# Up chunks 0 and 1 as a fourth seven-product pair in the last two token blocks, kept in DRAM in between

## The reference

```
xn = layernorm(x)
s  = silu(xn @ w_gate.T);  the k = 1376 smallest |s| of each token are set to 0
a  = (s * (xn @ w_up.T)) @ w_down.T
h  = relu(xn @ up_w) ** 2
r  = ((xn @ fc1_w) @ expert_w.T) * (sum of the 2 largest of xn @ gate_w)
y  = x + a + layernorm(h @ down_w + r @ fc2_w) * gamma + beta
```

## Time and profile before

| | us |
|---|---|
| median of 3 runs | 2335.4 |
| lowest, highest | 2333.67, 2336.62 |
| the profiled run, its own time | 2335.83 |
| its span in the trace | 2333.7 |
| TensorE busy | 2317.7 |
| VectorE busy | 1634.8 |
| ScalarE busy | 1086.9 |
| GpSimd busy | 829.3 |

### The profile page before, as it was taken

One profiled execution on the slowest core, in us unless ns is written; L12 is line 12 of the kernel. 1 busy time (PEld: TensorE's weight loads), 2 busy tenths in 40 slices (PEclk: granted clock), 3 DMA queues, 4 the chain that ended last, 5 costly groups with the idle time before them and its releaser, 6 DMA issues.

```text
span 2333.7 us, 27748 instructions
## 1 busy us (share of the span) xinstructions
PE 2317.7 (99%) x10504; PEld 1927.2 (83%) x10504; DVE 1634.8 (70%) x1810; ACT 1086.9 (47%) x1253; POOL 829.3 (36%) x682
## 2 busy tenths in 40 slices
PE   8999999999999999999999999999999999999999
PEld 6888888888877888888888888888888888888887
DVE  4349999976265989897334598898723568989850
ACT  3247776223233787722124387761213448785110
POOL 5467878796444021123024321304004413030500
PEclk9999999999999999999999999999999999999999
DMA  7798878878898666665778766665667865556555
GB/s 277 280 394 294 292 245 311 293 243 310 287 363 302 206 196 191 204 201 180 234 237 277 249 194 193 195 209 189 207 219 255 279 221 195 193 192 214 180 190 180
DMA packets 191047, 558.43 MB, mean 239 GB/s; under 512 B 20161, under 2 KB 29377, under 8 KB 190913
## 3 DMA queue, kind: packets, MB, share of 16 engines
q1 hardware_dynamic: 190912, 556.65, 71.0%
HBM read 429.62 MB, written 126.94 MB: 238 GB/s over the span
## 4 chain that ended last, share of the span: by engine, by line
PE 93%; DMA 3%; DVE 1%; SPq 1%; POOL 1%; ACT 0%; issue 0%; DVEq 0%; ACTq 0%
PE bank L945 30%; PE bank L947 30%; PE bank L946 30%; PE bank L965 2%; DMA mixed_w<-mixes 1%; DMA split_w<-w 1%; DMA w<-mixed_w 1%; PE bank L956 1%; POOL w L732 0%; SPq L565 0%; SPq L569 0%; PE bank L1038 0%; PE bank L1039 0%; DMA raw<-w_gate_dram 0%; POOL w L735 0%
## 5 line engine op out<-in xcount | busy, mean ns | idle before, releaser
L1292 DVE TENSOR_SCALAR_CACHE_REDUCE junk_v<-mag,cand 128x2816 bf16<-128x2816 f32 x248 | 780.3, 3146 | 8.8
L786 ACT ACTIVATE junk_s<-mag,cand 128x2816 uint8<-128x2816 f32 x248 | 655.4, 2643 | 222.2 <-DVE cand L1284 195.7
L945 PE MATMUL bank<-w,tok 128*128 128x512 f32 (+1 forms) x952 | 365.8, 384 | 1.8 <-DMA w<-split_w 1.7
L947 PE MATMUL bank<-w,tok 128*128 128x512 f32 (+1 forms) x952 | 364.3, 383 | 0.0
L946 PE MATMUL bank<-w,tok 128*128 128x512 f32 (+1 forms) x952 | 364.1, 382 | 0.0
L732 POOL TENSOR_TENSOR w<-raw,w 128x512 fp32r<-128x512 f32 (+1 forms) x196 | 268.1, 1372 | 77.5 <-ACT w L774 67.8
L945 PE MATMUL bank<-w,prod_t 128*128 128x512 f32 x672 | 269.4, 401 | 0.0
L947 PE MATMUL bank<-w,prod_t 128*128 128x512 f32 x672 | 262.8, 391 | 0.0
L946 PE MATMUL bank<-w,prod_t 128*128 128x512 f32 x672 | 261.9, 390 | 0.0
L945 PE MATMUL bank<-tok,w 128*128 128x512 f32 x640 | 249.0, 389 | 0.0
L946 PE MATMUL bank<-tok,w 128*128 128x512 f32 x640 | 249.0, 389 | 0.0
(11 more groups left out here) (149 smaller groups left out, 3728.3 us busy)
## 6 DMA issues: line engine op xcount, KB each, us to landing
w<-split_w SPq DMA_DIRECT2D x516, 512.0 KB, 3.5
split_w<-w SPq DMA_DIRECT2D x192, 512.0 KB, 4.9
w_more<-split_w SPq DMA_DIRECT2D x60, 512.0 KB, 5.2
w<-mixed_w SPq DMA_DIRECT2D x108, 256.0 KB, 3.5
rows<-x_dram SPq DMA_DIRECT2D x32, 512.0 KB, 4.9
raw<-w_down_dram SPq DMA_DIRECT2D x44, 256.0 KB, 3.9
raw<-w_up_dram SPq DMA_DIRECT2D x40, 256.0 KB, 3.1
w<-split_w SPq DMA_DIRECT2D x24, 392.0 KB, 3.5
```

Source lines behind the costliest of these rows:

```text
L786: act.activation(junk_s[:, :, :], mag[:, :, t, :], ACT.Sign, scale=-1.0, bias=cand[:, t:t + 1], accum_out=cnt[:, t:t + 1]).then_inc(counte ...
L945: pe.matmul(out, left[0], right[0], start=first, stop=False)
L947: return pe.matmul(out, left[1], right[0], start=False, stop=last)
L1292: dve.tensor_scalar(junk_v[:, :, :], mag[:, :, t, :], cand[:, t:t + 1], float(1 - (GATED - KEPT)), ALU.is_lt, ALU.add, accum_out=cnt[:, t: ...
```

## The change

- A fourth pair, up 0 and up 1, stands behind the third in blocks 2 and 3 (`FAST = [0, 3, 4, 4]`): 28 granules of 6 matmuls at 92 to 119 in place of 16 plain ones. Those blocks have 260 granules, and everything from latent to shared stands 28 further back: latent at 120, shared 2 and 3 at 184 to 199, up 2 at 200, up 3 at 208, out 0 at 216. The first turns stand after 211 to 214.
- The pair's results are written to `prod`, where the hidden values go next. At granule 123 SP spills both chunks to DRAM (`spilled_u`, 1 MB each) and at 199 loads them back. ScalarE's first read of hidden 0 waits for the spill.
- The two chunks get their sign in VectorE by one instruction of 2048 elements each, right before masks 0 and 1 (`sign_up`); before, it was part of the read.
- In blocks 2 and 3 sums 3 and 4 lie in `acc`, are split at granules 12 and 10 (before: 4 and 2) and wait for the stores of the block before.
- The search's first two steps stand at granules 101 and 108, inside the fourth pair, the others at 122 and on, 2.75 granules apart, the last settling at 202. Masks stand at 203, 204, 205, 207, 212 and 219, shared 3 is read at 203, up 2 at 211.
- The mixtures of the fourth pair are made in block 1 from granule 96 on: SP loads four raw granules to `raw`, one every second granule, GpSimd subtracts (four instructions), SP stores; four times, 18 granules apart.
- The third pair's raw granules are loaded in block 1 one at a granule, at 5 to 8, 10 to 13, 31 to 34 and 39 to 42 (before: eight at 8, four at 32, four at 40), mixed at 22, 30, 45, 53 (24, 32, 44, 52), stored as four transfers of 256 KB at 25, 33, 47, 55 (as one of 1 MB at 26, 34, 46, 54).

```diff
-PAIRS = [(("gate", 0), ("gate", 1)), (("gate", 2), ("gate", 3)), (("gate", GC - 2), ("up", GC - 2))]
-FAST = len(PAIRS)
+PAIRS = [(("gate", 0), ("gate", 1)), (("gate", 2), ("gate", 3)), (("gate", GC - 2), ("up", GC - 2)),
+         (("up", 0), ("up", 1))]
+FAST = [0, 3, 4, 4]
 FIRST_PAIRS = 2
+UP_PAIR, SPILLED_PAIR = 2, 3
 PRODUCTS = ["A11 B11", "S2 T2", "A12 B21", "S1 T1", "S4 B22", "S3 T3", "A22 T4"]
-PRODUCT_BANK = [[4, 6, 0, 2, 4, 6, 0], [2, 4, 6, 4, 6, 0, 2], [4, 6, 0, 4, 6, 0, 2]]
+PRODUCT_BANK = [[4, 6, 0, 2, 4, 6, 0], [2, 4, 6, 4, 6, 0, 2], [4, 6, 0, 4, 6, 0, 2],
+                [4, 6, 0, 4, 6, 0, 2]]
...
+        steps = [step for step in _middle + _last if step[0] not in sum(PAIRS[:FAST[b]], ())]
...
+        if later and FAST[b] > SPILLED_PAIR:
+            first = up_end + FAST_LAG + 4
+            steps_at = [first, first + 7]
+            steps_at += [last + 3 + (11 * k + 3) // 4 for k in range(BITS + 1 - len(steps_at))]
         else:
-            self.search_from = end[("gate", GC - 2)] + LAG + 1
-        self.search_at = {self.search_from + 3 * k: k for k in range(BITS)}
-        self.search_end = self.search_from + 3 * BITS
+            first = last + 5 if later else end[("gate", GC - 2)] + LAG + 1
+            steps_at = [first + 3 * k for k in range(BITS + 1)]
...
+        self.back_at = end[("shared", 3)] if FAST[b] > SPILLED_PAIR else None
+        read = {("up", c): self.back_at + 5 + 2 * c for c in range(2)} if self.back_at else {}
+        read.update({key: end[key] + LAG for key in end})
+        self.mask_at = {max(self.search_end + 1 + i, read.get(("up", g), 0) + 1): g
...
-MIX_LOADS = {8: range(8, 10), 32: range(10, 11), 40: range(11, 12)}
-MIX_AT = {24: 8, 32: 9, 44: 10, 52: 11}
-MIX_STORES = {26: 8, 34: 9, 46: 10, 54: 11}
+MIX_LOADS = {5 + i: (8, i) for i in range(4)}
+MIX_LOADS.update({10 + i: (9, i) for i in range(4)})
+MIX_LOADS.update({31 + i: (10, i) for i in range(4)})
+MIX_LOADS.update({39 + i: (11, i) for i in range(4)})
+MIX_AT = {22: 8, 30: 9, 45: 10, 53: 11}
+MIX_STORES = {25: (8,), 33: (9,), 47: (10,), 55: (11,)}
+LATE_MIXES = SPILLED_PAIR * HALF
+LATE_LOADS = {96 + 18 * n + 2 * i: (LATE_MIXES + n, i) for n in range(HALF) for i in range(4)}
+LATE_AT = {96 + 18 * n + 11: LATE_MIXES + n for n in range(HALF)}
+LATE_STORES = {96 + 18 * n + 14 + i: (LATE_MIXES + n, i) for n in range(HALF) for i in range(4)}
...
-SUMS_HI_AT = {2: 4, 4: 3}
-SUMS_LO_AT = {2: 4, 4: 3}
+SUMS_HI_AT = [{}, {2: 4, 4: 3}, {10: 4, 12: 3}, {10: 4, 12: 3}]
+SUMS_LO_AT = [{}, {2: 4, 4: 3}, {10: 4, 12: 3}, {10: 4, 12: 3}]
...
+        sums_acc = {i: [over(f"sums{i}_acc{part}", [P, HALF, 2 * P], F32R, acc_at + 8 * N * (2 * (i - 3) + part))
+                        for part in range(2)] for i in (3, 4)}
+        assert 32 * N == TILES * HID * 4
+        def sums_of(b, i):
+            return sums_acc[i] if i > 2 and FAST[b] > SPILLED_PAIR else sums[i]
...
+            def load_late_mix(n, i):
+                p, k = n // HALF, n % HALF
+                if n > LATE_MIXES:
+                    sp.wait_ge(late_stored, 64 * (n - LATE_MIXES))
+                src, width = words_of((PAIRS[p][i // 2], k + i % 2 * HALF))
+                sp.dma_start(raw[:, i, :], src).then_inc(late_loaded, 16)
+            def store_late_mix(n, i):
+                sp.wait_ge(late_mixes, 4 * (n - LATE_MIXES) + 4)
+                sp.dma_start(mixed_w[n, i], raw[:, i, :]).then_inc(late_stored, 16)
+            def spill(b, c):
+                for q in (4, 5) if c else (2, 6):
+                    for j in range(2):
+                        bank, value = emptied(b, ("fast", SPILLED_PAIR, q, j))
+                        sp.wait_ge(bank_emptied[bank], value)
+                sp.dma_start(spilled_u[c], prod[:, 4 * c:4 * c + 4, :, :]).then_inc(spilled[c], 16)
+            def load_back(b, c):
+                sp.wait_ge(spilled[c], 16 * spills(b))
+                sp.dma_start(prod[:, 4 * c:4 * c + 4, :, :], spilled_u[c]).then_inc(up_back[c], 16)
...
+                if plan.back_at:
+                    if m == plan.fast_end + 4:
+                        spill(b, 1)
+                        spill(b, 0)
+                    if m == plan.back_at:
+                        load_back(b, 0)
+                        load_back(b, 1)
...
+            def late_mix(n):
+                b11, b21, b12, b22 = (raw[:, i, :] for i in range(4))
+                at = 4 * (n - LATE_MIXES)
+                pool.wait_ge(late_loaded, 64 * (n - LATE_MIXES + 1))
+                pool.tensor_tensor(b11, b12, b11, ALU.subtract).then_inc(late_mixes, 1)
+                pool.tensor_tensor(b12, b22, b12, ALU.subtract).then_inc(late_mixes, 1)
+                pool.wait_ge(late_mixes, at + 1)
+                pool.tensor_tensor(b22, b22, b11, ALU.subtract).then_inc(late_mixes, 1)
+                pool.wait_ge(late_mixes, at + 3)
+                pool.tensor_tensor(b21, b21, b22, ALU.subtract).then_inc(late_mixes, 1)
...
+                if i > 2 and FAST[b] > SPILLED_PAIR:
+                    act.wait_ge(stored, 16 * (b * 2 * TILES + 1))
+                elif i > 2:
...
+                        if FAST[b] > SPILLED_PAIR and i == 0 and t == 0:
+                            for c in range(2):
+                                act.wait_ge(spilled[c], 16 * spills(b))
...
-            def sign_up(b):
-                ks = slice(4 * (GC - 2), 4 * (GC - 1))
-                dve.wait_ge(signs_done, b * (GC + 1) + PLANS[b].signs_before[GC - 2] + 1)
-                for j in range(2):
-                    for q in (4, 5):
-                        bank, value = emptied(b, ("fast", FAST - 1, q, j))
-                        dve.wait_ge(bank_emptied[bank], value)
+            def sign_up(b, g):
+                ks = slice(4 * g, 4 * g + 4)
+                dve.wait_ge(signs_done, b * (GC + 1) + PLANS[b].signs_before[g] + 1)
+                if g < 2:
+                    dve.wait_ge(up_back[g], 16 * spills(b))
+                else:
+                    for j in range(2):
+                        for q in (4, 5):
+                            bank, value = emptied(b, ("fast", UP_PAIR, q, j))
+                            dve.wait_ge(bank_emptied[bank], value)
                 dve.scalar_tensor_tensor(out=prod[:, ks, :, :], in0=positive[:, ks, :, :], scalar=-1.0,
                                          in1=prod[:, ks, :, :], op0=ALU.add, op1=ALU.mult).then_inc(up_signed, 1)
...
+                if (b, g) in SIGNED and g < 2:
+                    sign_up(b, g)
                 ks = slice(4 * g, min(4 * g + 4, GK))
                 for t in range(TILES):
-                    if b and g == GC - 2:
-                        dve.wait_ge(up_signed, b)
+                    if (b, g) in SIGNED:
+                        dve.wait_ge(up_signed, SIGNED.index((b, g)) + 1)
...
```

More of the change, by code:

```diff
@@ L110, with __init__ @@
 class Plan:
-    def __init__(self, later):
-        self.later = later
+    def __init__(self, b):
+        later = b > 0
         found = _plain(*_tail) if later else []
-        for p in range(FAST if later else FIRST_PAIRS):
+        for p in range(FAST[b] if later else FIRST_PAIRS):
             found += _fast_pair(p) if later else _first_pair(p)
-        steps = _middle + _last
+        steps = [step for step in _middle + _last if step[0] not in sum(PAIRS[:FAST[b]], ())]
         if not later:
@@ L136, in __init__ @@
                 self.end[g.key] = m
-        self.up0, self.out0, self.out1 = (self.start[key] for key in (("up", 0), ("out", 0), ("out", 1)))
-        end, up0, out0, out1 = self.end, self.up0, self.out0, self.out1
+        self.out0, self.out1 = (self.start[key] for key in (("out", 0), ("out", 1)))
+        end, out0, out1 = self.end, self.out0, self.out1
+        ups = end[("shared", 3)] + 1
         self.read_at = {end[key] + LAG: key for key in end if key[0] in ("gate", "latent", "routed", "shared")}
@@ L144, in __init__ @@
             self.read_at[end[_tail[0]] + FAST_LAG] = _tail[0]
[L146 to L147 removed]
+            last = self.fast_end = end["fast", FAST[b] - 1, len(PRODUCTS) - 1]
+            self.fast_at = {end["fast", p, q] + FAST_LAG: (p, q) for p in range(FAST[b]) for q in range(len(PRODUCTS))
                             if end["fast", p, q] + FAST_LAG < last + 2}
[L149 removed]
@@ L150, in __init__ @@
-            self.signs_at = {end["fast", p, q] + FAST_LAG + 3: (p, q) for p in range(FAST - 1) for q in (5, 6)}
-            self.signs_at[last + 4] = (FAST - 1, 6)
-            self.search_from = last + 5
-        else:
-            self.search_from = end[("gate", GC - 2)] + LAG + 1
-        self.search_at = {self.search_from + 3 * k: k for k in range(BITS)}
-        self.search_end = self.search_from + 3 * BITS
+            self.fast_at.update({last + 2: (FAST[b] - 1, 5), last + 3: (FAST[b] - 1, 6)})
@@ new lines, in __init__ @@
+            self.signs_at = {end["fast", p, q] + FAST_LAG + 3: (p, q) for p in range(UP_PAIR) for q in (5, 6)}
```

(20 more changed lines are left out.)

86 lines of the change are left out of this document (54 added, 32 removed).

## The result

The changed kernel takes 2346.5 us (median of 5 runs, 2345.0 to 2347.9); the kernel before 2335.05 us beside it. The ratio is 1.0049, with a 95% interval from 1.0035 to 1.0064: slower by 11.5 us, where 2351 was forecast. Its profiled run is the median one; the span is 2344.7 us, 11.0 over that of before.

A forecast was written before the change was run, and what follows sets the result against it. TensorE, busy 99% of the span, was taken as the bound: matmul pitch times count. From 2335.8 us, -10.9 + 21.6 + 3.6 + 2.0 - 1.0 = +15.3, so 2351; range 2336 to 2363.

The forecast's parts named there:

- What is removed: Up 0 and up 1 as a pair in blocks 2 and 3: 48 fewer matmuls on TensorE, -10.9 us.
- TensorE's arrival: TensorE reaches its first turn of `prod` at E+288.4 (E: third pair's end), 5.4 us earlier than before.
- The threshold: VectorE's search in the changed blocks ends at E+254.8, bounds E+252.8 and E+258, with 7.5 us of waits for ScalarE.
- Behind the threshold: VectorE's tie check, read of shared 3, masks and two signings (7.2 us) put up 2's first tile read at E+299.2.
- The wait: TensorE waits 10.8 us at the first turn in each of blocks 2 and 3 (bounds 8.1 and 13.3): +21.6.
- rival A: The work saved is paid out and VectorE keeps up, no wait at the turn: 2326 us; chance 0.12.
- The clock behind it: Slow matmuls on TensorE after each wait at the turn, 1.8 us per wait (bounds 0 and 2.2): +3.6.
- The sums at granule 12: Two low halves of sum 3 delay GpSimd's second word of T2, about 1.0 us in each of two blocks: +2.0.
- Block 1: Third pair's loads, spread and started earlier in block 1, cut TensorE's waits: -1.0 us, from -3.6 to +3.
- Signs: Expected in the profile: turn waits of some 10 us, search without idle, matmuls at 0.43 us, two signings over 3 us.
- At nothing: Spill, load back, fourth pair's transfers and conversions, late stores and subtractions priced as hidden, 0 to +2 us left for all.

The follow-up runs named there:

- the two runs: Changed kernel with three pairs in every later block: 2333.0 us; the same with the third pair's loads, mixing and stores at their former granules: 2335.9 us.
- The first and third experiment: Changed kernel with most of the tie check cut in blocks 2 and 3: 2322.8 us; changed kernel with up 2 read earlier, masks 2 and 3 later: 2323.0 us.
- the early read: Changed kernel with only the read of up 2 in blocks 2 and 3 moved from granule 211 to 205: 2334.2 us.
- the two passes: Kernel before the change with two VectorE passes of the signing's size put ahead of masks 0 and 1 in blocks 2 and 3: 2344.5 us.
- the old granules: Changed kernel with three pairs in every later block and the third pair loaded, mixed and stored at the granules of the kernel before: 2335.9 us.
- turns one granule later: Changed kernel with all turns one granule later (TURN_LEAD 4 for 5): 2340.9 us, 1.0021 of before.

## Why the prediction was right

The forecast was a wait of 8 to 13 us at the first turn of blocks 2 and 3, slower by 15 us; it is two waits of 9.1 and 9.4, slower by 11.5. The mechanism and its place are the forecast's; some of its terms came out by errors that cancel. By its steps:

- **What is removed**, -10.9: 48 matmuls went. The runs without the waits confirm it: 2322.8 and 2323.0, 12.6 and 12.4 us below before, which is 10.9 and block 1's 2.9 less what the sums cost.
- **TensorE's arrival**, E+288.4: it came at E+288.3.
- **The threshold**, E+254.8 within 252.8 to 258: it ends at 1579.93, E+253.2. I had left 7.5 us of waits for ScalarE; the list of VectorE's waits in the search has 4.5. Against E+254.2 before, the search is 1.0 us earlier: not its pace made VectorE late, but what stands behind it (+7.4 us).
- **Behind the threshold**: to the start of the read of up 2 the forecast has 43.7 us (298.5 less 254.8), and it took 43.7. That the sum is exact is luck. The signings were put at 3.6 each, 7.2, and took 3.38 and 2.28, 1.5 less; the sixteen masks were put at 17.0 and took 18.7, 1.7 more. The two errors cancel. The rule of the Trainium skill (SBUF — State Buffer, "Who interferes with whom") gave 3.55 for each signing; the trace agrees with the rule, and with 3.55 for the first signing alone. GpSimd's timeline of the changed kernel, one of its instructions around the start of each signing:

```profile
1606.54 1.47 POOL L867 TENSOR_TENSOR prod<-prod,mag 128x512 f32<-128x512 f32 x1
...
1614.89 3.25 POOL L867 TENSOR_TENSOR prod<-prod,mag 128x512 f32<-128x512 f32 x1 [1.29 <-DVE prod L1475]
```

The first signing starts at 1606.78, inside the first of these. The second starts at 1614.74, ahead of the other, and this time GpSimd's instruction is the long one.

- **The wait**, 10.8 each within 8.1 and 13.3: 9.1 and 9.4, 3.1 us less in all, which is the largest error of the sum. It is the 1.6 of the threshold, twice. The bounds take in only the signings and the masks; with the threshold's bounds too the lower one is 6.1, the figure that rival A goes by.
- **The clock behind it**, 1.8 each: 1.8 and 2.7 by the distance of turns 0 and 1 (5.01 and 5.89 for 3.20). By the Trainium skill (TensorE: Matmul & The Clock Gate, Part 1) idling brings the half-rate clock back; the trace agrees, with the granted clock at 0.50. Behind shorter waits the runs show both levels.
- **The sums at granule 12**, +2.0: the list of waits has 0.6 for the second word and 0.5 for VectorE's read, the medians 1.4, the late starts of the two traces 1.3 and 0.6. So the size was about right. TensorE wanted the second word at 1217.8 (1221.17 less the 3.4 it was ahead) and started at 1218.56, 0.8 late where some 1.0 was forecast; the second wait was not in the forecast.
- **Block 1**, -1.0: it is -2.9 by the medians of the two runs, -2.8 by the traces from block 0's first turn to block 1's. The mechanism (spread loads) was named, its size was too small: I priced it by listed waits alone.
- **Signs**: the wait, its place, its releaser and the slow matmuls were as said. Two were not: only one signing took over 3 us, and the search was not without idle.
- **At nothing**: spill, load back, late mixtures, stores. The first and third experiment show that this held. Each 1 MB of the spill and the load back landed 5.9 to 9.3 us after its issue.

The sum from the traces, by how late or early the same matmuls start: -0.6 up to block 0's first turn, -2.8 from there to block 1's, +1.3 and +0.6 in the first products of blocks 2 and 3, -10.9 for the matmuls, +11.1 and +12.3 at the first turns with the slow matmuls behind them. That is +11.0, the whole difference of the spans. The turns' 23.4 are 0.4 more than the list's 18.5 and 4.5, since the list leaves out the first tenths of each wait.

## What to carry to other kernels

Where one engine is busy 99% of the time, look in each stage for the instruction that it asks for with the smallest margin. A saving on the bound engine takes its whole size off that margin, and every instruction added ahead of it in the other engine's queue takes more: here 2.6 us of margin met 5.4 us saved and 6.4 us added (7.4 behind the threshold, less the 1.0 by which the threshold came earlier). Move what the bound engine asks for first ahead of what it asks for later: the same instructions in another order went from 0.5% slower to 0.5% faster.

## What the runs showed of the hardware

- The granted clock fell to 0.50 behind every wait of 6.4 to 9.4 us. Behind shorter ones it did either: it stayed at 1.00 behind 1.7 (the kernel before, block 1), 2.5 (the early read, block 2) and 2.7 us (the two passes, block 3), and fell behind 1.8 (the old granules, block 1), 2.0 (turns one granule later, start of block 2), 2.7 (the two passes, block 2) and 2.8 us (the early read, block 3). So a wait of 2 us may already be followed by slow matmuls, and the same wait need not be in the next block. Behind a wait at the turn they cost 1.6 to 2.7 us, on top of the wait.
- In the changed kernel a signing of 2048 elements took 2.28 us where it started with GpSimd idle, and 3.38 where it started 1.2 us ahead of the end of an instruction of GpSimd's. GpSimd's instruction that started 0.15 us behind the first kind took 3.25 us; beside the masks the same form took 1.5 to 1.7.
